# A fused recurrence and gated-attention layer on one core: the routing logits formed from halves kept in fp16, four column tiles at once

## What is computed

```
x = silu(x_prev * conv_w[:, 0] + x * conv_w[:, 1])       # h, after a layernorm
q = silu(x @ Wq); k = x @ Wk; v = x @ Wv; g = x @ Wg
q, k = rotary(q), rotary(k)
logits = einsum('bhld,hdr->bhlr', v, router_w)           # two routes for each token and head
scores = softmax(logits); onehot = one_hot(argmax(scores), 2)
norm = 1 / cumsum(onehot)                                # tokens of the same route so far
qk = (q * scores * onehot * norm) (k * onehot)^T * tril  # only tokens of one route see each other
o = layernorm_per_head(qk @ v)
out = (silu(g) * o) @ Wout
```

## Time and profile before

| | us |
|---|---|
| median of 3 runs | 1799.89 (1796.76 to 1800.38) |
| the profiled execution's own time | 1798.36 |
| its span, first to last instruction | 1796.4 |
| PE busy | 1640.6 (91%) |
| DVE busy | 1472.1 (82%) |
| ACT busy | 740.3 (41%) |
| POOL busy | 631.1 (35%) |
| mean granted clock of TensorE | 0.963 |

### The profile page before, as it was taken

How to read it: one execution, slowest core, us unless ns; L and a number is a source line. 1 busy time by engine, 2 the same in 40 slices (tenths; PEclk the granted TensorE clock), 3 DMA queues, 4 the chain that set the end, 5 groups by cost and what they waited for, 6 DMA issues and landing times.

```text
span 1796.4 us, 38777 instructions
## 1 busy us (share of the span) xinstructions
PE 1640.6 (91%) x15767; PEld 876.3 (49%) x15799; DVE 1472.1 (82%) x2004; ACT 740.3 (41%) x933; POOL 631.1 (35%) x716
## 2 busy tenths in 40 slices
PE   0345999999999999999999989999999999999996
PEld 0123555554555545555555545555555545555553
DVE  7898888887788978887798877888888877889832
ACT  5735434443444333443434434444344344443420
POOL 2412344344333343443234344323433433334321
PEclk9867999998999989999999999999999999999998
DMA  9400011111101101111010111110011111001000
GB/s 271 177 12 24 13 28 33 36 37 37 37 25 27 32 27 37 36 36 38 16 33 25 36 37 36 36 30 23 22 37 36 36 37 36 25 25 29 20 13 24
DMA packets 23430, 71.00 MB, mean 40 GB/s; under 512 B 2256, under 2 KB 2512, under 8 KB 23248
## 3 DMA queue, kind: packets, MB, share of 16 engines
q1 hardware_dynamic: 23248, 68.37, 13.2%
HBM read 51.59 MB, written 16.78 MB: 38 GB/s over the span
## 4 chain that ended last, share of the span: by engine, by line
PE 87%; DVE 8%; issue 3%; ACT 1%; POOL 0%; DMA 0%; SPq 0%; POOLq 0%; DVEq 0%; ACTq 0%
PE ps_g L387 25%; PE ps_g L388 24%; PE ps_g L391 24%; PE ps_t L482 4%; PE ps_o L539 4%; PE ps_t L379 3%; PE ps_o L379 2%; DVE big L779 2%; PE ps_t L524 1%; DVE seg L827 1%; PE ps_s L524 1%; DVE big L796 0%; DVE seg L818 0%; DVE small L808 0%; DVE big L317 0%
## 5 line engine op out<-in xcount | busy, mean ns | idle before, releaser
L387 PE MATMUL ps_g<-big,h_hi 128*128 128x512 f16 x1536 | 590.2, 384 | 16.7 <-DVE small L922 11.0
L388 PE MATMUL ps_g<-big,h_hi 128*128 128x512 f16 x1536 | 589.9, 384 | 0.0
L391 PE MATMUL ps_g<-big,h_lo 128*128 128x512 f16 x1536 | 589.3, 384 | 0.0
L387 PEld LDWEIGHTS ps_g<-big,h_hi 128*128 128x128 f16 x1536 | 159.5, 104 | 171.5 <-issue 15.8
L391 PEld LDWEIGHTS ps_g<-big,h_lo 128*128 128x128 f16 x1536 | 151.6, 99 | 186.7 <-issue 9.2
L1153 POOL TENSOR_TENSOR small<-small 128x1 f32<-128x1 f32 x64 | 14.2, 221 | 634.2 <-DVE small L812 625.3
L388 PEld LDWEIGHTS ps_g<-big,h_hi 128*128 128x128 f16 x1536 | 151.5, 99 | 167.9 <-issue 8.0
L387 PE MATMUL ps_g<-big 128*128 128x512 f16 x512 | 195.5, 382 | 0.7 <-DVE big L888 0.6
L1172 POOL TENSOR_TENSOR vx<-vx,ek 128x1024 f32<-128x1024 f32 x32 | 76.4, 2386 | 337.6 <-ACT ek L611 325.4
L388 PE MATMUL ps_g<-big 128*128 128x512 f16 x512 | 194.9, 381 | 0.0
L391 PE MATMUL ps_g<-big 128*128 128x512 f16 x512 | 194.9, 381 | 0.0
(11 more groups left out here) (157 smaller groups left out, 2967.7 us busy)
## 6 DMA issues: line engine op xcount, KB each, us to landing
x_ring<-in_x SPq DMA_DIRECT2D x32, 512.0 KB
vx<-in_ctx SPq DMA_DIRECT2D x32, 512.0 KB
out<-x_ring SPq DMA_DIRECT2D x32, 512.0 KB
big<-in_wv SPq DMA_DIRECT2D x2, 2048.0 KB, 21.4
big<-in_wg SPq DMA_DIRECT2D x2, 2048.0 KB, 20.8
big<-in_wout SPq DMA_DIRECT2D x2, 2048.0 KB, 20.1
big<-in_wq SPq DMA_DIRECT2D x1, 2048.0 KB, 14.1
big<-in_wk SPq DMA_DIRECT2D x1, 2048.0 KB, 19.5
```

What stands on the lines that cost most here:

```text
L387: nc.tensor.matmul(dst[:, :], hi, hi_of(u)[:, kc * HALF:(kc + 1) * HALF], start=(kc == 0), stop=False)
L388: nc.tensor.matmul(dst[:, :], hi, lo_of(u)[:, kc * HALF:(kc + 1) * HALF], start=False, stop=False)
L391: last = nc.tensor.matmul(dst[:, :], lo, hi_of(u)[:, kc * HALF:(kc + 1) * HALF], start=False, stop=(kc == KC - 1))
```

## The change

The logits become fp16 work. At the start, DVE scales `w_route` and splits it into two fp16 halves, `w_route_hl`, 32 columns for each of the 8 chunks (16 upper, 16 lower). In each step `route_products` makes 16 fp16 products: the halves of `w_route` are the loaded weights (128x32), the 128 columns of h move (`h_hi`, then `h_lo`), and chunk kc goes to the column tile kc mod 4, that is to rows 32 (kc mod 4) onward of `ps_t[1]`. ACT copies the 128x128 result to SBUF (`copy_logits`), and one fp32 product with `r_sum` (128x16) adds the tiles and halves, undoes the scale and turns the result to tokens by heads (`route_logits`). It stands in columns 128 to 143 of `ps_t[1]`.

Order: on PE the products stand behind the projection of q, the folding product behind that of k, and `sign_sums` moves behind v0. On DVE `signs` moves from between the two parts of the denominator to behind the rotation of q, and `denominator_terms` no longer waits for the logits of step i. On ACT `copy_logits` takes the place of `route_prob`, which moves behind the copy of k.

```
@@ small
-        small = sb("small", [P, 373])
+        small = sb("small", [P, 378])
+        r_max, r_bound, r_scale, r_inv = col(1), col(1), col(1), col(1)
+        r_sum = col(H)
@@ PE, step
-                    if not opening(i):
-                        route_logits(i)
                     project(ps_g[0], h_hi, h_lo, UQ, s_qp, 1)
...
+                    if not opening(i):
+                        route_products(i)
                     project(ps_g[1], h_hi, h_lo, UK, s_kp)
                     if opening(i):
                         for r in range(5, 9):
                             bound_row(r)
-                        pe.wait_ge(s_wroute, 8)
-                        route_logits(i)
-                    sign_sums(i)
+                        pe.wait_ge(s_rw, 8)
+                        route_products(i)
+                    route_logits(i)
                     project(ps_g[0], h_hi, h_lo, UV, s_vp)
+                    sign_sums(i)
@@ PE
+            def route_products(i):
+                after(pe, s_hlo, 2 * (i + 1))
+                for a in (h_hi, h_lo):
+                    for kc in range(KC):
+                        rows = slice(kc % 4 * 2 * H, (kc % 4 + 1) * 2 * H)
+                        last = nc.tensor.matmul(ps_t[1][rows, 0:P], w_route_hl[:, kc * 2 * H:(kc + 1) * 2 * H],
+                                                a[:, kc * P:(kc + 1) * P], start=(a is h_hi and kc < 4),
+                                                stop=(a is h_lo and kc >= 4))
+                last.then_inc(s_dlp, 1)
             def route_logits(i):
-                after(pe, s_h, i + 1)
-                for kc in range(KC):
-                    last = nc.tensor.matmul(ps_t[1][:, 0:H], fa[:, kc * P:(kc + 1) * P], w_route[:, kc * H:(kc + 1) * H],
-                                            start=(kc == 0), stop=(kc == KC - 1))
-                last.then_inc(s_dl, 1)
+                after(pe, s_dlc, i + 1)
+                nc.tensor.matmul(ps_t[1][:, P:P + H], logits_t, r_sum, start=True, stop=True).then_inc(s_dl, 1)
@@ ACT, step
                     A(q_sb, ps_g[0][:, :], ACT.Silu, scale=inv[:, UQ:UQ + 1]).then_inc(s_q, 1)
                     if not opening(i):
-                        route_prob(i)
+                        copy_logits(i)
                     act.wait_ge(s_kp, i + 1)
                     A(k_sb, ps_g[1][:, :], ACT.Copy, scale=inv[:, UK:UK + 1]).then_inc(s_k, 1)
                     if opening(i):
-                        route_prob(i)
+                        copy_logits(i)
+                    route_prob(i)
@@ ACT
+            def copy_logits(i):
+                act.wait_ge(s_dlp, i + 1)
+                after(act, s_dl, i)
+                A(logits_t, ps_t[1][:, 0:P], ACT.Copy).then_inc(s_dlc, 1)
@@ DVE, step
                     denominator_terms(n)
-                if main:
-                    signs(i)
-                if nxt:
                     denominator_scan(n)
...
                     rotate(dve, V, i, 0, q_sb, rot_q, s_r1q, s_rq)
+                    signs(i)
                     if opening(i):
                         lo_unit(4)
@@ DVE, denominator_terms
                 after(dve, s_pre, n)
-                after(dve, s_dl, n)
@@ DVE, the start: r_max behind tokens_by_time(), split_route_weights() behind the last route_chunk
+            V.tensor_reduce(r_max, x_ring[:, 2, :], AX_X, ALU.max, apply_absolute_value=True).then_inc(s_rw, 1)
+            def split_route_weights():
+                V.tensor_reduce(r_sum, ident[:, :].rearrange("p (j h) -> p h j", h=H), AX_X, ALU.add).then_inc(s_rw, 1)
...
+                V.tensor_scalar(r_bound, r_max, mx[:, UV:UV + 1], mx[:, UV + 1:UV + 2], ALU.mult, ALU.max).then_inc(s_rw, 1)
...
+                V.tensor_scalar(r_bound, r_bound, TINY, None, ALU.max).then_inc(s_rw, 1)
...
+                V.reciprocal(r_scale, r_bound).then_inc(s_rw, 1)
...
+                V.tensor_scalar(r_scale, r_scale, W_TOP, None, ALU.mult).then_inc(s_rw, 1)
+                V.tensor_scalar(r_inv, r_bound, mx[:, U:U + 1], LN_BOUND / (W_TOP * H_TOP), ALU.mult, ALU.mult)\
+                 .then_inc(s_rw, 1)
...
+                V.tensor_scalar(r_sum, r_sum, r_inv, None, ALU.mult).then_inc(s_rws, 1)
+                V.tensor_scalar(hl[:, :, 0, :], rows, r_scale, None, ALU.mult).then_inc(s_rws, 1)
...
+                V.scalar_tensor_tensor(hl[:, :, 1, :], rows, r_scale, hl[:, :, 0, :], ALU.mult, ALU.subtract)\
+                 .then_inc(s_rw, 1)
```

More of the change, by code:

```diff
@@ L128, in flamingo_layer @@
         w_route = turn[:, P:2 * P]
+        w_route_hl = turn[:, 2 * P:3 * P].bitcast(F16)
+        logits_t = turn[:, 3 * P:4 * P]
         q_sb = work[:, 4 * C:4 * C + HALF]
@@ L224, in flamingo_layer @@
         s_qt, s_kt = sem("qt_copied"), sem("kt_copied")
-        s_dl = sem("route_logits")
+        s_dlp, s_dlc, s_dl = sem("logits_matmul"), sem("logits_copied"), sem("route_logits")
+        s_rw, s_rws = sem("route_weights"), sem("route_weights_scaled")
         s_wprod, s_wroute, s_wmean, s_wcentred = (sem(n) for n in
@@ L684, in route_prob @@
                 after(act, s_cf, i)
-                A(pr, ps_t[1][:, 0:H], ACT.Abs).then_inc(s_th, 1)
+                A(pr, ps_t[1][:, P:P + H], ACT.Abs).then_inc(s_th, 1)
                 act.wait_ge(s_th, 2 * i + 1)
@@ L788, in route_chunk @@
                  .then_inc(s_wroute, 1)
+            def split_route_weights():
+                V.tensor_reduce(r_sum, ident[:, :].rearrange("p (j h) -> p h j", h=H), AX_X, ALU.add).then_inc(s_rw, 1)
+                dve.wait_ge(s_rw, 2)
+                dve.wait_ge(s_wsc, UV + 2)
+                V.tensor_scalar(r_bound, r_max, mx[:, UV:UV + 1], mx[:, UV + 1:UV + 2], ALU.mult, ALU.max).then_inc(s_rw, 1)
+                dve.wait_ge(s_rw, 3)
+                V.tensor_scalar(r_bound, r_bound, TINY, None, ALU.max).then_inc(s_rw, 1)
+                dve.wait_ge(s_rw, 4)
+                V.reciprocal(r_scale, r_bound).then_inc(s_rw, 1)
+                dve.wait_ge(s_rw, 5)
+                V.tensor_scalar(r_scale, r_scale, W_TOP, None, ALU.mult).then_inc(s_rw, 1)
+                V.tensor_scalar(r_inv, r_bound, mx[:, U:U + 1], LN_BOUND / (W_TOP * H_TOP), ALU.mult, ALU.mult)\
+                 .then_inc(s_rw, 1)
+                dve.wait_ge(s_rw, 7)
+                dve.wait_ge(s_wroute, 8)
+                hl = w_route_hl.rearrange("p (k s h) -> p k s h", s=2, h=H)
+                rows = w_route.rearrange("p (k h) -> p k h", h=H)
+                V.tensor_scalar(r_sum, r_sum, r_inv, None, ALU.mult).then_inc(s_rws, 1)
+                V.tensor_scalar(hl[:, :, 0, :], rows, r_scale, None, ALU.mult).then_inc(s_rws, 1)
+                dve.wait_ge(s_rws, 2)
+                V.scalar_tensor_tensor(hl[:, :, 1, :], rows, r_scale, hl[:, :, 0, :], ALU.mult, ALU.subtract)\
+                 .then_inc(s_rw, 1)
             def centre(u):
@@ L909, in signs @@
                 after(dve, s_cump, i)
-                V.tensor_scalar(sgn, ps_t[1][:, 0:H], 0.0, 2.0, ALU.is_ge, ALU.mult).then_inc(s_sgp, 1)
+                V.tensor_scalar(sgn, ps_t[1][:, P:P + H], 0.0, 2.0, ALU.is_ge, ALU.mult).then_inc(s_sgp, 1)
                 dve.wait_ge(s_sgp, i + 1)
@@ L1110, in _ @@
             tokens_by_time()
+            dve.wait_ge(s_base, 1)
+            V.tensor_reduce(r_max, x_ring[:, 2, :], AX_X, ALU.max, apply_absolute_value=True).then_inc(s_rw, 1)
             lo_unit(0)
@@ L1127, in _ @@
                 route_chunk(m)
+            split_route_weights()
             centre(UV + 1)
```

## The result

The changed kernel takes 1787.29 us (median of 5 runs, 1785.36 to 1790.81), the kernel before 1800.38 beside it (5 runs, 1796.76 to 1803.24). The ratio is 0.9929, 95% interval 0.9914 to 0.9944: faster, by 13 us (0.7%), where 7 were forecast. The profiled execution of the changed kernel is one of its longest (own time 1790.71, span 1788.7), and against the profiled one of before (1798.36, span 1796.4) it gains 7.7.

What follows compares the result with a forecast made beforehand. PE bounds the kernel, but its gain turns into a wait on POOL. Opening +4.05, 24 ordinary steps +5.3, six behind jumps -15.6, last step -1.2: together -7.5 from 1799.9, said as 1793 us, range 1766 to 1814 (forecast case's own 1787 to 1798).

Steps and rivals of the forecast that it cites:

- PE gives 1.16 and can use at most 0.2 of it: Ordinary step: PE's own step falls from 49.93 to 48.8 us, but the next chain allows only 0.21.
- L922's slack of 0.21: Ordinary step: the chain from the transposes of x through DVE to the first route coefficient has 0.21 us to spare.
- Sixteen products, taken 0.5 between 0.26 and 1.6: On PE, the new fp16 logit products, without a profile row, take 0.5 us a step, bounds 0.26 and 1.6.
- The signs late, the alternation 9.03: Later signs make POOL and DVE alternate for 9.03 us; PE waits 1.4 for rotated k, ordinary step 50.15.
- the 6.26 called POOL's undisturbed pace: Lower bound for POOL's work up to rotated k, 6.26 us, which would make PE the bound again.
- Rival 3: Ordinary steps: POOL and DVE interleave better, PE stays the bound, 48.9 us a step, total 1763; chance 0.14.
- Behind the jumps, 2.6 each: Six steps behind jumps back: less PE work and an earlier clock rise save 2.6 us each, 15.6 together.
- The opening, +4.05: Until step 1: scaling and splitting the weights, then DVE waiting for ACT in step 0, add 4.05 us.
- The clock in the new wait: Ordinary steps: the 1.4 us gap before the transposes of rotated k shouldn't take PE's clock down.
- 2 (the clock gives nothing back): Behind the jumps: half-speed stretch ends at the same moment, six steps give only 1.2 each, total 1801; chance 0.21.
- 4: Ordinary steps: the POOL and DVE alternation costs more, rotated k 0.6 us later, total 1807; chance 0.18.
- 5: Ordinary steps: the clock falls in the new wait, 24 steps lose about 1.7 us each, total 1833; chance 0.04.

Runs made afterwards that it cites:

- e3: New fp16 products at the step's head, folding product behind q, signs where the kernel before had them; 1799.7 us.
- e8: e7 with the gated output's low half ahead of the residual and its statistics on DVE; 1757.2 us.
- e2: Changed kernel with the signs ahead of DVE's rotation of q instead of behind it; 1782.6 us.
- e1: Changed kernel with POOL rotating k before it spreads the route signs; 1786.9 us.
- e4: e3 with all route coefficients ahead of the numerator's recurrence on DVE; 1829.6 us.
- e7: e6 with the first route coefficient instruction alone ahead of the numerator on DVE; 1774.4 us.
- e5: Changed kernel with the eight old fp32 products kept as well at the step's head, result unused; 1826.1 us.
- e6: e3 with the sixteen products between the two halves of q's projection; 1781.8 us.
- e10: e8 run again, beside e9; 1758.2 us.
- e9: Kernel before, old fp32 products, with only two moves: first coefficient ahead of the numerator, gated output's low half ahead of the residual; 1799.6 us.

## Why the prediction was right, point by point

- **PE gives 1.16 and can use at most 0.2 of it: right.** The order of chains behind PE held to a tenth. DVE's own slack of 1.52 showed as 1.63 of idle before L1048 in the changed kernel; L922's slack of 0.21 showed in e3, where the signs stand in their old place: the step is 49.78, and 49.93 - 0.21 is 49.72.
- **Sixteen products, taken 0.5 between 0.26 and 1.6: 0.34.** The nearest row was that of the small tiles. The fold was 0.14 as forecast. With PE as the bound (e8) the step is 1.13 shorter than 49.93, where 1.80 - 0.34 - 0.14 makes 1.32; 0.18 of the other 0.19 are the two joins shown at e8. So two misses nearly cancel in the 1.16 of the point above: the products are 0.16 cheaper than taken, and the joins, which the prediction put at nothing, cost 0.15 to 0.2.
- **The signs late, the alternation 9.03: 9.08.** Even the pieces came close: POOL's L1259 1.05 for 1.0, its L318 1.27 for 1.26, the step 50.17 for 50.15. The rule of the Trainium skill cited there (SBUF - State Buffer, Who interferes with whom) lets whichever engine came first hold the shared ports for its whole instruction, and the trace agrees: the two engines took turns. e2 adds the other half, that the same instruction costs 0.68 where it doesn't meet the other engine. One bound was misread: the 6.26 called POOL's undisturbed pace spans 907.47 to 913.73, where DVE was at its own rotation; with DVE idle the same five instructions take 5.00 (125.09 to 130.09 in the changed kernel's step 0). The forecast itself didn't use it.
- **The step behind it that I had not named:** with POOL out of the way, `sign_sums` (e1), the coefficient (e2, e3) and the gated output's low half (e4, e7) each bind at 49.89, 49.70 to 49.78, and 49.57. Rival 3 priced the step at 48.9 with L922 as the only other bound. The chain from the transposes of x through DVE to `gt_lo` was not in my reading; it binds at 49.57 (e7), so rival 3's 48.9 and its 1763 could not have come from a better interleaving alone. It took e8's two moves.
- **Behind the jumps, 2.6 each: 2.5 each,** but as five times 3.4 and once -1.7. The mechanism (the clock rises sooner because dense products begin 3.4 us earlier) is seen in the windows: half the clock for 6 to 8 dense products and no slow stretch of L482 ahead of them, for 6 to 13 with it. e5 shows it by experiment: old products at the head again cost 5.0 each. The size is less sure. The five are 0.8 better than forecast, and the second stand in the sixth was no part of it, so that this trace's sum agrees is luck. e1 has the same head and no second stand: its six steps are 14.7 us shorter than before, 2.5 each, with the full rate 3.6 to 5.8 us behind the restart. In e2, the same head again, it is 1.8 each. And L482's 3.59 us was not the clock alone: at three of the six jumps of the kernel before PE stood a second time in front of its last record, for 0.2 to 1.2 us.
- **The opening, +4.05: +2.97.** The stall in step 0 was there and cost 1.3 (forecast 1.0 after the rest). The term too large was the prologue: 1.70 for 3.05. The split itself took 2.12 and r_max 1.0; but a small DVE instruction of the prologue, L798 before and L842 after, took 1.64 us at 77.05 before and 0.20 at 78.06 after. The rows show why: before, POOL's L1180 ran from 76.29 to 78.63 and L798 ended at 78.69, 0.06 behind it; after, POOL's had ended at 77.40, ahead of L842. No run varies this by itself. The prediction's own figures, 126.93 and 131.1, are 4.17 apart, not 4.05. e2, e3 and e6, with the signs sooner in step 0, have the first mark of step 1 at 168.2 to 168.7, 0.8 to 1.4 ahead of the changed kernel's 169.55: that is the size of the step 0 term.
- **The clock in the new wait: no fall,** as forecast. 23 waits of up to 1.3 us, and a granted clock of 1.00 in all 23 ordinary steps.
- **The rivals.** 2 (the clock gives nothing back) fell with the ledger, 3 with PE's 23 waits, 4 and 5 with the step's length. The median, 1787.3, lies at the lower edge of the forecast's own range. Of the 13.1 us between the medians the ledger explains 7.7; 3.4 more is the distance of the profiled execution of after from its median, with the second stand in it, and 2.0 that of before from its own.

## What to carry to other kernels

When an instruction is made cheaper, list every chain that closes within the saving, and for each the last link that someone waits for; here two lay within 0.4 us of PE's step and a third was made by the change itself; the saving was worth 13 us, and with the products and their results placed anew and two short moves, which by themselves showed no gain, 41. Judge where to put a result by when it meets another engine's work and who waits behind it: waiting for an input can cost nothing if the time would have gone into a collision. At the head of a loop's body put long instructions, not short ones: here that was worth 18 us (e6 against e3).

## What the runs showed of the hardware that I had not expected

- **Behind a jump back PE can stand twice, and the second stand comes behind a fixed count of instructions.** The first gap is 3.2 to 3.8 us in every kernel (4.1 to 4.6 in e5). With sixteen short products at the head (e3, e4) a second one of 2.4 to 6.2 us follows behind the eleventh product, 0.35 to 0.5 us after the restart, at all twelve jumps. With 512-column products at the head (the changed kernel, e1, e2, e6, e7, e8, e10) it comes at three of 42, each time behind the tenth or eleventh product, 2.3 to 3.6 us after the restart: 2.58 in the changed kernel, 3.97 in e7, 0.97 in e8. With the old products at the head it comes in front of the sixteenth record, 1.8 to 3.4 us after the restart: at three jumps of six in the kernel before (0.2, 1.2, 1.1), at four in e9 (0.5 to 3.0), at none in e5. It looks as though instructions come in batches, and as though a head that is used up fast waits for the next one. That reading fits all of these, but only the placement was tested. The Trainium skill (Runtime: NRT & Kernel Launch, Instruction fetch mechanics) says that a taken branch outside the held window forces a fetch before execution goes on; the first gap agrees with it, the second it doesn't mention.
- **Sixteen products in four column tiles take 0.34 us, 21 ns each,** with 128 columns moving in each and a weight load apiece. Each way of switching costs no more than 0.1 us: 0.07 to 0.09 into the tiles (0.21 behind L503 for 0.14, 0.31 for 0.22 in e8), some 0.09 out of them (the second eight take 0.21 to the next dense product, the first eight 0.13).
- **A small DVE instruction can wait out a large GpSimd one:** 1.14 us for 0.11 (e4's L977), so that even sixteen-column work has a price by its place, where GpSimd is at work beside it.
- **Where the clock falls at a jump back differs from jump to jump.** Behind the restart at 840.03 two products run at the full rate (0.39, 0.38), the third takes 0.49 and the next 0.63; the gap of 3.26 us ahead of them still has a granted 1.00. At 1453.72 it is five. At 431.74 the clock has fallen inside the gap (0.50 from 431.1 to 431.7) and the first product takes 0.60. In e8, behind a gap of 3.34 us at 625.40, it doesn't fall at all (a granted 1.00 from 620 to 640).
